# Last output tile of a two-layer FFN kernel: half groups and pre-scaled weights, and a later start of GpSimd's first weight sums

## The reference

```
x = x + ffn0(cond0(x))
x = x + ffn1(cond1(x))
```

```
W[o, i] = q[o, i] * s[o, i // 128]
out = (silu(x Wg.T) * (x Wu.T)) Wd.T
```

## Time and profile before

| | us |
|---|---|
| median of 3 runs | 655.27 |
| lowest, highest | 654.75, 655.49 |
| profiled execution | 654.61 |
| its span | 652.7 |
| busy: PE, PEld, DVE, ACT, POOL | 630.5, 519.4, 469.3, 332.4, 254.7 |
| granted clock of PE over the span | 0.988 |

### The profile page before, as it was taken

One profiled execution on the slowest core, in us unless ns is written; L12 is line 12 of the kernel. 1 busy time (PEld: TensorE's weight loads), 2 busy tenths in 40 slices (PEclk: granted clock), 3 DMA queues, 4 the chain that ended last, 5 costly groups with the idle time before them and its releaser, 6 DMA issues.

```text
span 652.7 us, 7964 instructions
## 1 busy us (share of the span) xinstructions
PE 630.5 (97%) x2868; PEld 519.4 (80%) x2868; DVE 469.3 (72%) x564; ACT 332.4 (51%) x440; POOL 254.7 (39%) x197
## 2 busy tenths in 40 slices
PE   8979999999999989999999999999999999999993
PEld 6868888888878868888888888887877887888872
DVE  5885564526457998885337787647669999999995
ACT  5785634334445444543114454335457885578842
POOL 4650010000000046753023665430003898969886
PEclk9979999999999989999999999999999999999998
DMA  8520113101021101421011111130122121221102
GB/s 251 158 66 2 48 50 101 63 20 43 20 72 32 33 33 40 146 97 57 33 43 54 37 61 57 55 57 18 60 74 92 61 85 65 81 79 59 56 33 96
DMA packets 22473, 42.27 MB, mean 65 GB/s; under 512 B 9524, under 2 KB 10548, under 8 KB 22388
## 3 DMA queue, kind: packets, MB, share of 16 engines
q1 hardware_dynamic: 20388, 38.56, 18.8%
q0 software_dynamic: 2048, 3.22, 1.8%
HBM read 39.67 MB, written 2.10 MB: 64 GB/s over the span
## 4 chain that ended last, share of the span: by engine, by line
PE 86%; ACT 5%; DVE 3%; SPq 2%; issue 1%; DMA 1%; POOL 0%; POOLq 0%; DVEq 0%; ACTq 0%
PE ps_down L1574 6%; PE ps_down L1575 6%; PE ps_down L1576 6%; PE ps_up L1574 4%; PE ps_up L1575 4%; PE ps_up L1576 4%; PE ps_gate L1679 3%; PE ps_m L1732 3%; PE ps_gate L1732 3%; PE ps_gate L1681 3%; PE ps_m L1733 3%; PE ps_gate L1680 3%; PE ps_gate L1574 3%; PE ps_gate L1575 3%; PE ps_down L1733 3%; PE ps_gate L1733 3%
## 5 line engine op out<-in xcount | busy, mean ns | idle before, releaser
L669 POOL TENSOR_TENSOR w_total<-w_raw 128x512 f32<-128x512 f32 x13 | 17.0, 1310 | 161.7 <-DVE x_lo L1102 127.0
L1574 PE MATMUL ps_down<-act_hi,w_hi 128*128 128x512 f32 (+1 forms) x180 | 70.7, 393 | 1.0 <-DVE xp L1398 1.0
L1576 PE MATMUL ps_down<-act_hi,w_lo 128*128 128x512 f32 (+1 forms) x180 | 70.2, 390 | 0.0
L1575 PE MATMUL ps_down<-act_lo,w_hi 128*128 128x512 f32 (+1 forms) x180 | 70.2, 390 | 0.0
L703 POOL TENSOR_TENSOR up_sum<-up_sum,up_more 128x1024 f32<-128x1024 f32 x14 | 33.8, 2413 | 67.0 <-DVE up_more L1214 67.0
L1102 DVE TENSOR_TENSOR w_lo<-w_raw,w_hi 128x512 fp32r<-128x512 f32 (+4 forms) x45 | 48.3, 1074 | 13.3 <-ACT w_hi L766 9.2
L766 ACT ACTIVATE w_hi<-w_raw 128x1024 fp32r<-128x1024 f32 (+4 forms) x30 | 27.0, 900 | 45.4 <-DVE w_raw L1109 22.8
L678 POOL TENSOR_TENSOR act_lo<-up,act_hi 128x512 fp32r<-128x512 f32 x14 | 18.2, 1301 | 68.6 <-ACT act_hi L924 42.6
L1102 DVE TENSOR_TENSOR b_rows<-b_raw,b_hi 32x1024 fp32r<-32x1024 f32 (+2 forms) x30 | 31.8, 1060 | 18.3 <-ACT b_rows L783 14.2
L1574 PEld LDWEIGHTS ps_down<-act_hi,w_hi 128*128 128x128 f32 (+1 forms) x180 | 33.8, 188 | 8.1 <-DVE w_lo L1102 1.4
L1576 PEld LDWEIGHTS ps_down<-act_hi,w_lo 128*128 128x128 f32 (+1 forms) x180 | 33.8, 188 | 7.3
(11 more groups left out here) (254 smaller groups left out, 1877.3 us busy)
## 6 DMA issues: line engine op xcount, KB each, us to landing
w_int<-in_ffn_gu SPq DMA_DIRECT2D x14, 512.0 KB, 3.5
w_raw<-in_ffn_gu SPq DMA_DIRECT2D x13, 512.0 KB, 3.5
w_raw<-in_cond_gu SPq DMA_DIRECT2D x9, 512.0 KB, 3.2
w_raw<-in_ffn_dn SPq DMA_DIRECT2D x8, 448.0 KB, 3.2
w_int<-in_ffn_dn SPq DMA_DIRECT2D x8, 448.0 KB, 3.2
xp<-in_x SPq DMA_DIRECT2D x8, 256.0 KB, 5.2
xp<-in_x SPq DMA_DIRECT2D x1, 2048.0 KB, 10.2
out_t<-xp SPq DMA_DIRECT2D x8, 256.0 KB, 2.0
```

Source lines behind the costliest of these rows:

```text
L1574: nc.tensor.matmul(ps[0:m, :], w_hi[0:r, s, cols], rhs_hi(k, r), start=start and n == 0, stop=False)
L1575: nc.tensor.matmul(ps[0:m, :], w_hi[0:r, s, cols], rhs_lo(k, r), start=False, stop=False)
L1576: last = nc.tensor.matmul(ps[0:m, :], w_lo[0:r, s, cols], rhs_hi(k, r), start=False, stop=stop and n == len(ks) - 1)
```

## The change

The last down tile (part 1, tile 3) is computed in two ways. For the first token half, its seven groups (now named "l") are half groups: 2 matmuls of 512 columns each, in half a PSUM tensor (`last_bank`), ScalarE reads group 0, VectorE adds groups 1 to 6, in turns to `down_sum` and straight to `xp`, then one add joins the two. For the second half, the tile's weights are loaded a second time before (`last_q`), turned into float, multiplied by their scales (`last_weights`, with the scales spread to all partitions by SyncE: `s_row`, then `s_wide`), and split into hi and lo; PE forms the whole sum over seven groups with 21 matmuls in one PSUM bank (`last_rest`), and VectorE adds it to `xp` once. GpSimd has no part in this tile any more.

The weights are prepared in cond1: loads between the other SyncE loads, ScalarE's and VectorE's instructions at tiles 0 and 2. The two output transfers of the tile wait for `last_sum` 1 and 2. Apart from that, GpSimd's first weight sums (tile 1 of ffn0) wait for all nine x sums instead of the eighth x piece.

```diff
@@ -113,7 +114,10 @@
             for k in ks:
-                add(n + o, "d", k, "a" if k in (0, 2) or (part, o, k) == (1, HK - 1, 4) else "v")
+                if (part, o) == (1, HK - 1):
+                    add(n + o, "l", k, "a" if k == 0 else "v")
+                else:
+                    add(n + o, "d", k, "a" if k in (0, 2) else "v")
     return groups
@@ -193,7 +197,14 @@
         up_more = place("up_more", [P, 2, TOK], F32, at["w"])
-        down_last = place("down_last", [P, TOK], F32, at["w"] + 8 * KB)
+        last_q = place("last_q", [P, ACT_TILES * P], I32, at["act_hi"] + 24 * KB)
+        last_f = place("last_f", [P, ACT_TILES * P], F32, at["act_hi"] + 20 * KB)
+        s_wide = place("s_wide", [P, P * ACT_TILES], F32, at["lora0"] + 12 * KB)
+        s_row = place("s_row", [1, P * ACT_TILES], F32, at["lora0"] + 28 * KB)
+        last_cut = 4 * P
+        last_hi, last_lo = ([place(f"last_{part}{n}", [P, size], F32R, where) for n, (size, where) in
+                             enumerate(zip((last_cut, ACT_TILES * P - last_cut), places))]
+                            for part, places in (("hi", (at["w"] + 10 * KB, at["w"] + 14 * KB)), ("lo", (at["lora0"] + 36 * KB, at["mask"]))))
         down_sum = place("down_sum", [P, 3, TOK], F32, at["t"])
@@ -276,7 +287,9 @@
         more_added, out_sum = sem("more_added"), sem("out_sum")
-        last_added, last_sum = sem("last_added"), sem("last_sum")
+        s_row_in, s_wide_in, last_in = sem("s_row_in"), sem("s_wide_in"), sem("last_in")
+        last_f_done, last_scaled, last_hi_done, last_ready = sem("last_f_done"), sem("last_scaled"), sem("last_hi_done"), sem("last_ready")
+        rest_ready, last_sum = sem("rest_ready"), sem("last_sum")
         sum_done = sem("sum_done")
@@ -365,14 +378,19 @@
+        def last_bank(n):
+
+            bank = group_banks[(len(groups) - ACT_TILES + n // 2) % len(group_banks)]
+            return bank[:, chunk(n % 2)]
+
         def group_bank(g):
-            return group_banks[g.m % len(group_banks)]
+            return last_bank(g.k) if g.name == "l" else group_banks[g.m % len(group_banks)][:, :]
...
             part, j = divmod(g.n, ACT_TILES + HK)
-            if g.name == "d":
+            if g.name in ("d", "l"):
                 col = (j - ACT_TILES) * NT1 + ACT_TILES * part + g.k
@@ -380,6 +398,10 @@
             return s_group[:, j, col:col + 1]
+
+        def last_part(part):
+
+            return slice(0, last_cut) if part == 0 else slice(last_cut, ACT_TILES * P)
@@ -571,6 +593,12 @@
                                      allow_slow_non_contiguous=True).then_inc(s_in, 16)
+                    sp.wait_ge(seven_done, 7 * 2 * ACT_TILES)
+                    col = (HK - 1) * NT1 + ACT_TILES
+                    sp.dma_start(s_row[:, :].rearrange("a (p k) -> a p k", k=ACT_TILES),
+                                 d["ffn1_down_s"][:, col:col + ACT_TILES].rearrange("(a p) k -> a p k", a=1)).then_inc(s_row_in, 16)
+                    sp.wait_ge(s_row_in, 16)
+                    sp.dma_start(s_wide[:, :], s_row[:, :].unsqueeze(1).to_broadcast([1, P, P * ACT_TILES])).then_inc(s_wide_in, 16)
                 if ph.name == "ffn0 down a":
@@ -594,6 +622,9 @@
                         load_tile(ph, o // 2, o % 2)
+                        if ph.name == "cond1" and o == 2:
+                            sp.wait_ge(down_ready, ph.d0)
+                            sp.dma_start(last_q[:, :], d["ffn1_dn"][1, HK - 1]).then_inc(last_in, 16)
                         if ph.name == "cond down b" and o == 1:
@@ -612,7 +643,7 @@
                     else:
-                        sp.wait_ge(last_sum, 2 * c + 2)
+                        sp.wait_ge(last_sum, c + 1)
                     sp.dma_start(out[o][:, chunk(c)], xp[:, o, chunk(c)]).then_inc(out_done, 16)
@@ -663,7 +694,7 @@
                 if q == 1:
-                    pool.wait_ge(x_ready, x_count(3, 1))
+                    pool.wait_ge(x_summed, len(x_sums))
                 pool.wait_ge(seven_done, 7 * (q if j == 0 else q - 1))
@@ -722,15 +753,6 @@
-            def last_sums(n, m, o):
-                here = xp[:, o, :]
-                pool.wait_ge(dve_read, group_of[n, "d", 1].ev)
-                nc.gpsimd.tensor_tensor(here, here, down_sum[:, m % 3, :], ALU.add).then_inc(more_added, 1)
-                pool.wait_ge(more_added, m + 1)
-                pool.wait_ge(dve_read, group_of[n, "d", 3].ev)
-                for c in range(CH):
-                    nc.gpsimd.tensor_tensor(here[:, chunk(c)], here[:, chunk(c)], down_more[m % 3][:, chunk(c)], ALU.add).then_inc(last_added, 1)
-
             for part in range(2):
@@ -741,7 +763,6 @@
                     down_sums(part, o)
-            last_sums(2 * (ACT_TILES + HK) - 1, 2 * HK - 1, HK - 1)
@@ -854,7 +875,7 @@
                 act.wait_ge(group_ready, g.m + 1)
-                nc.scalar.activation(out_, group_bank(g)[:, :], ACT.Copy, scale=group_scale(g)).then_inc(act_read, 1)
+                nc.scalar.activation(out_, group_bank(g), ACT.Copy, scale=group_scale(g)).then_inc(act_read, 1)
@@ -885,8 +906,15 @@
                     integers(n + 2)
-                if m == 2 * HK - 1:
-                    scaled(group_of[n, "d", 4], down_last[:, :])
+
+            def last_tile(n, m):
+                act.wait_ge(out_sum, m - 2)
+                scaled(group_of[n, "l", 0], down_sum[:, m % 3, chunk(0)])
+
+            def last_weights_hi():
+                for part in range(2):
+                    act.wait_ge(last_scaled, 1)
+                    nc.scalar.activation(last_hi[part][:, :], last_f[:, last_part(part)], ACT.Copy).then_inc(last_hi_done, 1)
@@ -1031,6 +1059,10 @@
                         tile_hi(ph, o // 2 + 1, o % 2)
+                    if ph.name == "cond1" and o == 0:
+                        act.wait_ge(last_in, 16)
+                        nc.scalar.activation(last_f[:, :], last_q[:, :], ACT.Copy).then_inc(last_f_done, 1)
+                        last_weights_hi()
                     if ph.name == "cond1":
@@ -1084,8 +1116,9 @@
                     group_tile(n + j, ACT_TILES * part + j, j > 0)
-                for o in range(HK):
+                for o in range(HK - part):
                     group_down(n + ACT_TILES + o, part, o)
+            last_tile(2 * (ACT_TILES + HK) - 1, 2 * HK - 1)
@@ -1208,10 +1241,10 @@
-            def added(g, here, tokens=slice(0, TOK)):
+            def added(g, here):
                 dve.wait_ge(group_ready, g.m + 1)
-                return nc.vector.scalar_tensor_tensor(out=here, in0=group_bank(g)[:, tokens], scalar=group_scale(g), in1=here,
+                return nc.vector.scalar_tensor_tensor(out=here, in0=group_bank(g), scalar=group_scale(g), in1=here,
                                                       op0=ALU.mult, op1=ALU.add)
@@ -1260,21 +1293,33 @@
-            def group_down_last(n, m, o):
-
-                here = xp[:, o, :]
-                dve.wait_ge(act_read, group_of[n, "d", 0].ea)
-                added(group_of[n, "d", 1], down_sum[:, m % 3, :]).then_inc(dve_read, 1)
-                dve.wait_ge(act_read, group_of[n, "d", 2].ea)
-                added(group_of[n, "d", 3], down_more[m % 3][:, :]).then_inc(dve_read, 1)
-                dve.wait_ge(act_read, group_of[n, "d", 4].ea)
-                added(group_of[n, "d", 5], down_last[:, :]).then_inc(dve_read, 1)
-                dve.wait_ge(dve_read, group_of[n, "d", 5].ev)
-                for c in range(CH):
-                    added(group_of[n, "d", 6], down_last[:, chunk(c)], chunk(c)).then_inc(last_sum, 1)
-                    dve.wait_ge(last_added, c + 1)
-                    dve.wait_ge(last_sum, 2 * c + 1)
-                    nc.vector.tensor_tensor(here[:, chunk(c)], here[:, chunk(c)], down_last[:, chunk(c)], ALU.add).then_inc(last_sum, 1)
+            def last_tile(n, m):
+
+                both, (here, rest) = down_sum[:, m % 3, chunk(0)], (xp[:, HK - 1, chunk(c)] for c in range(CH))
+                dve.wait_ge(act_read, group_of[n, "l", 0].ea)
+                added(group_of[n, "l", 1], both).then_inc(dve_read, 1)
+                dve.wait_ge(out_sum, HK)
+                added(group_of[n, "l", 2], here).then_inc(dve_read, 1)
+                for k, before, to in ((3, 2, here), (4, 1, both), (5, 3, here), (6, 4, both)):
+                    dve.wait_ge(dve_read, group_of[n, "l", before].ev)
+                    added(group_of[n, "l", k], to).then_inc(dve_read, 1)
+                dve.wait_ge(dve_read, group_of[n, "l", 6].ev)
+                nc.vector.tensor_tensor(here, here, both, ALU.add).then_inc(last_sum, 1)
+                dve.wait_ge(rest_ready, 1)
+                nc.vector.tensor_tensor(rest, rest, last_bank(ACT_TILES), ALU.add).then_inc(last_sum, 1)
+
+            def last_weights():
+
+                dve.wait_ge(s_wide_in, 16)
+                dve.wait_ge(last_f_done, 1)
```

(40 more changed lines are left out.)

## The result

| | before | after |
|---|---|---|
| median, us | 655.38 | 663.70 |
| lowest, highest, runs | 654.75, 656.85, 4 | 663.44, 664.14, 4 |
| span of the profiled execution | 652.7 | 662.2 |

The ratio of the times is 1.0124, interval 1.0106 to 1.0143: the change makes the kernel slower by 8.3 us. The forecast was 649.7 with a range of 647.4 to 660.4: a gain was forecast, a loss came, and it lies above the range.

A forecast was written before the change was run, and what follows sets the result against it. PE, busy 97% of the span, was taken as the bound, so edits count only at its waits, low clock or end. Terms -4.6 - 1.0 + 0 = -5.6 us gave 649.0, median 649.7; range 647.4 to 660.4.

The forecast's parts named there:

- the length of the spread: SyncE's copy of the scales' row from one partition to all 128 (448 KB): 6.2 us, no loss.
- the upper bound, 24.9: Longest time in us for the spread, if each of the four partitions had only a quarter of the pack_raw rate.
- The rule of the Trainium skill: Eight partitions share one port of about 27.2 GB/s: spread an estimated 16.9 us, median 660.1.
- The threshold: Spread's data may last until 437.5, 6.4 us, before a_raw and b_raw are late for ScalarE at 438.12.
- rival B: Spread takes 7 to 11 us, or small loads slip through late: +0.6 to +4.6, 650.3 to 654.3; chance 0.18.
- Rival A: Spread holds the DMA engines, a_raw and b_raw stand behind it; at 15.5 us, path moves 9.0, 658.7; chance 0.22.
- Small packets of one queue may slip between those of another: Argument against rival A: small loads might pass the spread on the DMA engines; no size given.
- The last tile, -4.6: End of kernel: VectorE ends 5.3 us earlier, outputs cost 0.7; -4.6 us, bounds -5.4 and -3.8.
- The 0.7 for the outputs in a row: Kernel's end: four output transfers stand in a row, costing 0.7 us, between 0 and 0.9.
- The first sums, -1.0: GpSimd's later wait around 230 us: -1.8 or, if the clock falls, -0.1; taken -1.0, bounds -3.6 and +1.5.
- rival C: Only GpSimd's wait fails: VectorE's later pieces late, low clock back, -0.1 to +1.5, 650.6 to 652.2; chance 0.10.
- The arithmetic, 0: New weights' preparation on ScalarE and VectorE in cond1 is hidden: cost 0, bounds 0 and +0.8.

The follow-up runs named there:

- e7: Kernel before plus only the s_row load and a spread from one partition to 64 partitions (224 KB), data unused: 661.49 us, one run.
- e8: Kernel before plus only the s_row load and a spread from one partition to 32 partitions (112 KB), data unused: 654.89 us, one run.
- e6: Changed kernel with scales read from HBM, laid out group by group, and GpSimd's old wait for its first weight sums: 650.31 us, ratio 0.9940.
- e1: Changed kernel, but SyncE sends the spread only after GpSimd's a_raw and b_raw loads have landed: 649.99 us, ratio 0.9927.
- e3: Kernel before plus only the s_row load, the spread to all partitions and VectorE's wait for it, data unused: 670.30 us, ratio 1.0240.
- e5: Changed kernel with scales read from HBM and laid out group by group, so VectorE's product reads without a stride: 649.28 us, ratio 0.9923.
- e2: Changed kernel with each partition's copy of the scales read from one HBM row, s_row and its wait dropped: 649.16 us, ratio 0.9916.
- e4: Kernel before with only GpSimd's first weight sums waiting for all nine x sums: 655.34 us, ratio 1.0006.

## Why the prediction was wrong

**The step that failed** is the length of the spread, "I take 6.2, no loss". It is 18.6 us. The 6.2 came from twelve pack_raw loads of 36 KB "each onto four partitions", one every 0.5 us. But no two of those in a row go to the same partitions (L652 writes rows 0 to 3, then 4 to 7, then 8 to 11, and so on), so 0.5 us can be the rate at which several groups together take data, and not what one group does; only loads in a row to one and the same group would have shown that. And they write, where the spread reads. Which of the two made 6.2 too short was not tried. The row was the nearest to be had and still bounded nothing; the upper bound, 24.9, held.

The rule of the Trainium skill that the prediction weighed and set aside ("look faster than that rule") gave the better size: its estimate of 16.9 us is within 1.7 of the measured landing, and with the fixed 1.8 of e7 and e8 it would be 18.7.

**The threshold was right within 1 us.** The prediction let the spread's data flow for 6.4 us, 7.2 from its issue, before anything was late. e8 with 6.0 from its issue lost nothing, and e7 with 10.2 lost 4.0 of idling, so that 6.2 would have been free. e7 also stands for rival B (7 to 11 us, +0.6 to +4.6): its idling is in that range, its time with the low clock is not.

**Rival A's mechanism was right, its size too small.** It named the order: spread, a_raw, ScalarE, w_raw, w_hi, w_lo, PE; the chain shows exactly this. With 15.5 us it gave 658.7; the time was 663.7. By the rule of the Trainium skill it would have been 660.1. Its stall of 9.0 became 12.3: the spread is issued at 431.45 and not 430.3, since s_row must land first (+1.2), and lands 18.6 later where rival A had 0.8 and 15.5 (+2.3); a_raw lands 1.0 behind it and not 0.6 (+0.4), and ScalarE itself comes for a_raw 0.8 later (438.88 for 438.12, from the start-up and the first sums, -0.8), together +3.1 at ScalarE, and +3.3 at PE. The low clock after the idle, +1.5, was in no rival. So +4.8 is missing there; the last tile gave 0.3 more, and the remaining 0.5 of the 5.0 is within what the runs differ by. "Small packets of one queue may slip between those of another" did not happen.

**The last tile, -4.6:** -4.9 in the profile, 4.3 by e6. PE's last matmul was forecast 7.7 and VectorE's last add 8.8 behind the tile's start; both are so. The join add waits behind GpSimd's add of tile 2, as worked out (it takes 1.30 for 0.7). The 0.7 for the outputs in a row was 0.4 (3.6 for 3.2).

**The first sums, -1.0:** right by luck. The gap is 1.83 where 1.95 was forecast, and the queue of waits is as worked out. But -1.0 was the middle of two ends, -1.8 if the clock stays up and -0.1 if it falls, and neither end came out: it is -1.0 where the clock stayed up (four profiles) and +0.2 where it fell (e1, 33.50 for 33.34). Tile 1 starts only 1.5 earlier (237.90 with the start-up taken off, for 239.40), and 0.5 of that is lost again before its own scale matmuls, of which PE's timeline shows 0.15 as a wait for VectorE's part_sum. And a fall of the clock, priced at 1.7, costs 0.9 in the old place (33.34 - 32.49) and 1.2 in the new (33.50 - 32.34). Against a kernel before whose clock stays up, as in e3, the wait gives 0.15. Of rival C, e1 has the low clock back, at +0.2 within its -0.1 to +1.5.

**The arithmetic, 0:** 0. The product took 1.89 and not 1.09, not quite the doubling that the prediction priced at 0.4 late; it cost nothing (e5).

Without the failed step the forecast stands, with the luck of the -1.0 in it: e2 and e5 have 649.2 and 649.3, where 649.7 was said. e1 (650.0) and e6 (650.3) beat both kernels too, and the intervals of these four overlap. e1 shows that moving the spread behind two waits repairs it as well.

## What to carry to other kernels

Copying data from one partition to all is a read of one partition, and its time here went by what was written (18.5, 10.2 and 6.0 us for 128, 64 and 32 copies), not by the one row read: keep such a row in HBM and read it from there for every partition. A long DMA can delay small urgent ones behind it on its own queue and on another (SyncE's and GpSimd's here), so ask of each new transfer what is issued within its duration and who waits for that with no slack. A rate taken from loads in a row is a bound only if they use the same partitions and the same direction; if a slow transfer can't be excluded, put it behind the urgent loads, where it cost nothing here (e1). And compare a small gain by a trace only between profiles at the same clock: the 1.0 of the first sums was 0.15.

## What the runs showed of the hardware that was not expected

- A read from one partition runs at 27.3 to 27.6 GB/s over and above a fixed 1.8 us, between 32, 64 and 128 partitions written (one profile each for 32 and 64). From HBM the same row, read 128 times, lands in 5.1 to 5.4 us (e2, e5, e6). Whether a partition or its group's port is the limit was not tried: a row cut over two partitions of a group and of two groups would tell.
- While it runs, a load of 32 KB on another queue waits for practically the whole of it (18.1 us for 18.6; 9.8 for 10.2 in e7), not for its share. That it is the DMA engines it waits for is read from their share of 0.90; a load to partitions away from the spread's source was not tried.
- A VectorE product of 896 columns takes 1.89 to 1.91 us if its second operand has a stride of seven elements (after, e1, e2), 1.09 if it has none (e5, e6).
- Gaps of about 2 us on PE bring the low clock in one execution and not in another. The gap of 1.83 before tile 1 left it at 1.00 in the kernel after, but not in e1; and the gap of 2.21 before product 5 left it at 0.56 before, but not in e3. The two windows, of e1 and then of e3:

```profile
239.20:242.60 3.40, 3.34 (x8) 2.66 (x9) 3.30 (x6) 0.59 (x2) 0.00 (x0) 0.54 0.22 45
```
```profile
234.70:238.00 3.30, 3.28 (x15) 2.48 (x15) 3.20 (x6) 2.39 (x6) 0.00 (x0) 1.00 0.00 0
```

  8 matmuls in 3.4 us in the one, 15 in 3.3 in the other. The traces price such a fall at 0.9 to 1.2 us and show a start-up that moves by up to 2 us for a cause that stays open. Both feed the spread of the run times; whether they make up all of e4's 6 us isn't shown.
